# Expert selection, the last projection and the shared expert's groups put in another order at the end of an attention and expert layer

## The chip, the cores and the metric

The kernel runs on one core of a Trainium2 chip. The metric is the time of one execution on the device in microseconds (us), the median of several runs. TensorE (PE) multiplies matrices, VectorE (DVE) does most of the elementwise work, ScalarE (ACT) the activations and many copies, GpSimd (POOL) a part of the elementwise work and the indirect DMAs, and SyncE (SP) issues most DMAs.

## What is computed

One layer for x of shape (2, 2048, 256): attention with a memory that is updated by segments of 64 tokens, and then a mixture of 32 experts beside a shared expert. Abridged:

```python
# attention: 16 heads of 128, one step for each 64 tokens
scores = where(causal, q k^T / sqrt(128), -inf)
att_dot = softmax(scores) @ v
att_mem = sigma(q) @ mem / (sigma(q) @ z)          # sigma = elu + 1
delta = v - sigma(k) @ mem / (sigma(k) @ z)
mem += sigma(k)^T @ delta;  z += sum(sigma(k))
x = x + (beta * att_mem + (1 - beta) * att_dot) @ Wo      # on layernorm(x)

# experts, on n = layernorm(x), 4096 tokens
scores = sigmoid(n @ gate_w.T); sc = scores + gate_bias
groups = the 2 best of 4 groups of 8 experts, by the sum of their two best sc
topk_idx = the 4 best sc in these groups; weights = 2 * scores / sum(scores)
# each expert takes its first CAP = 64 tokens in the order of the tokens
out[token] += weight * (silu(n w1) * (n w3)) w2
shared = silu(n @ shared_gate) * (n @ shared_up) @ shared_down
x = x + out + shared
```

So of the tokens that choose an expert only the earliest 64 are kept. That makes the selection a search for the 64 earliest tokens of each of 32 experts.

## The kernel before

**Attention.** The 4096 tokens are 16 blocks (`NBLK`) of 128 tokens of both batches, and the 16 heads are 8 groups (`NG`) of 2. The main loop (`body` on each engine) goes over 16 blocks x 8 groups = 128 steps; step n = 8 x block + group, and the last block is steps 120 to 127. A step on PE: `numerators` for segment 0, the key projection of the next step (L1305), `attended_transposes` of the step before, `update` (L1364), the query projection, `numerators` for segment 1 (L1354), `probability_transposes`, the value projection, `key_transposes`, `update` for segment 1, `attend` (L1381), `scores` (L1328). DVE runs in its own fixed order: after `state(n, g, 0)` comes `sigma_k` of the next step (L875), `delta(n, 1)`, `sigma_q` (L868), `state(n, g, 1)` (L902), and PE's next `numerators` wait for that `state` (`mem_ready`). Pieces of the block before hang in between: in group 0 PE's output projection (`project_out`, L1410, 64 matmuls), in group 1 the residual and the statistics of the second layernorm, then the normalisation, the gate's chain of small operations, in group 7 its weights and `picks`.

**Picks.** For each block `picks` writes, for each expert and token, the value 4096 - token if the token chose the expert and 0 if not; a DMA stores them in DRAM (`picks`, 32 x 4096). The earliest 64 are then the 64 largest. `top8` finds eight of them by a MAX8 and strikes them out by a MATCH_REPLACE (which the trace shows as two instructions), and `ROUNDS` = 8 such rounds give 64. Before the change the selection comes after all blocks: four quarters of the tokens side by side on 128 partitions (`vq`, 1024 values, L1056 and L1057), then a merge of the four lists (`cm`, 256 values on 32 partitions).

**Shared expert.** It runs in 8 groups of 2 blocks. In the traces one group is, on PE, four `shared_half` (gate and up for two halves fc, L1462: banks bank_q, bank_k, chain_k, chain_q) and one `shared_down` (L1481), on ACT two `shared_silu` (L744), on DVE two `shared_mul` (L1044) and two `shared_add` (L1050) into `acc`, which holds x after attention. `FRONT` = 7 groups run before the experts, beside gate and selection, one after them. **Experts** run in 16 pairs: POOL gathers the rows of a pair, PE, ACT and DVE compute them (columns L1498, up L1510, down L1526), POOL adds them to DRAM (`expert_sums`) by indirect scatters (L586), two at a time, each two waiting for the two before. At the end SP loads the sums (`yt`, L431), DVE adds them to `acc` (`sum_add`, L1276, 4 pieces), SP stores the output (L436).

**What sets the order.** All of it is written out by hand. Each engine executes its list in order and waits on semaphores; SP's DMAs are issued in order too. `w_hi` and `w_lo`, the projection weights, share their memory with all buffers of the second half (`shared_place`), so the loads of shared weights and columns wait until the projections of some groups have run (`v_mm`). The expert weights lie over the attention's buffers (`expert_place`), so their loads wait for the end of attention.

## Time and profile before

| | us |
|---|---|
| median of 3 runs | 1823.87 |
| lowest and highest | 1821.38, 1825.12 |
| the profiled execution | 1825.59 |
| its span from first to last instruction | 1823.7 |

| engine | busy share of the span |
|---|---|
| PE matmuls | 95% |
| DVE | 66% |
| POOL | 50% |
| ACT | 44% |

The granted TensorE clock is 0.987 of full speed over the span. The profile page also cuts the span into 40 slices; PE is at 9 tenths or more in all but the first slice and three late ones (8 tenths in two, 3 tenths in the last). A time of a row is counted from the start of the span. A bracket behind a row of the timeline gives how long the engine had been idle before it, and who released it.

### The profile page before, as it was taken

What the parts mean: (1) busy time and instruction counts of PE and PEld (TensorE: products, weight loads), DVE (VectorE), ACT (ScalarE), POOL (GpSimd) and SP (SyncE); (2) the same over time, 40 slices, a digit from 0 to 9 for tenths busy, and PEclk for the clock granted to TensorE, in tenths of its full rate; (3) what the DMA queues carried; (4) which work ended last, traced back from release to release, by engine and by line L of the source; (5) the groups of instructions that cost most, each with busy time, mean ns of one, the idle gap of its engine ahead of it and who ended that gap; (6) DMA issues with size and microseconds to landing.
All of it is one profiled execution on the core that took longest, in us unless ns stands there. A gap on an engine that the chain in (4) does not pass through costs nothing. (4 is left out here: it accounts for less than half of the span.)

```text
span 1823.7 us, 45885 instructions
## 1 busy us (share of the span) xinstructions
PE 1728.6 (95%) x17990; PEld 1473.8 (81%) x17990; DVE 1208.0 (66%) x3996; ACT 805.4 (44%) x1936; POOL 916.7 (50%) x830
## 2 busy tenths in 40 slices
PE   6999999999999999999999999999999999989893
PEld 5788888888888888888888888888888888866451
DVE  6766757575767767575767677675767675663852
ACT  3544535353535445353535354453535354541040
POOL 3655646464646546464646455454646464530162
PEclk8999999999999999999999999999999999999997
DMA  4200000100000000001000000000010000046747
GB/s 152 70 22 25 15 19 8 32 8 25 15 15 25 15 25 15 19 8 32 8 22 18 15 25 15 25 15 19 8 32 8 15 25 9 25 148 188 207 80 202
DMA packets 83190, 75.23 MB, mean 41 GB/s; under 512 B 20992, under 2 KB 73808, under 8 KB 82720
## 3 DMA queue, kind: packets, MB, share of 16 engines
q1 hardware_dynamic: 79264, 65.89, 11.9%
q0 software_dynamic: 3680, 6.40, 1.9%
q8 instruction: 144, 2.36, 0.5%
q14 instruction: 70, 0.57, 0.1%
q10 hardware_dynamic: 32, 0.01, 0.0%
HBM read 47.78 MB, written 24.47 MB: 40 GB/s over the span
## 5 line engine op out<-in xcount | busy, mean ns | idle before, releaser
L489 POOL TENSOR_TENSOR step_place<-step_place 128x512 f32<-128x512 f32 x128 | 169.7, 1326 | 243.5 <-ACT step_place L645 243.5
L659 ACT ACTIVATE step_place<-chain_q,step_place 128x128 f32<-128x128 f32 x512 | 159.9, 366 | 275.2 <-DVE step_place L886 274.9
L902 DVE TENSOR_TENSOR step_place<-step_place,chain_k 128x258 f32<-128x258 f32 x256 | 107.7, 421 | 260.7 <-PE chain_q L1364 260.6
L525 POOL TENSOR_TENSOR step_place<-step_place 128x256 f32<-128x256 f32 x128 | 78.8, 615 | 313.5 <-DVE step_place L1079 313.5
L1410 PE MATMUL bank_o<-step_place 128*128 128x256 f32 x1024 | 226.0, 379 | 0.0
L480 POOL TENSOR_SCALAR step_place<-step_place 128x512 f32<-128x512 f32 x128 | 191.0, 1492 | 44.0 <-ACT step_place L639 43.9
L1410 PEld LDWEIGHTS bank_o<-step_place 128*128 128x128 f32 x1024 | 192.3, 190 | 25.4 <-issue 0.5
L474 POOL TENSOR_SCALAR step_place<-step_place 128x512 f32<-128x512 f32 x128 | 190.3, 1486 | 0.3 <-POOL step_place L498 0.3
L1354 PE MATMUL chain_k<-step_place 128*64 128x129 f32 x2048 | 166.0, 282 | 20.3 <-DVE step_place L902 20.2
L1364 PE MATMUL chain_k<-step_place 64*128 64x129 f32 x1024 | 181.4, 297 | 1.8 <-ACT step_place L659 1.1
L1364 PE MATMUL chain_q<-step_place 64*128 64x129 f32 x1024 | 181.6, 297 | 0.0
L1364 PEld LDWEIGHTS chain_k<-step_place 64*128 64x128 f32 x1024 | 132.4, 186 | 44.8 <-issue 42.3
L498 POOL TENSOR_TENSOR step_place<-step_place 128x512 f32<-128x512 f32 x128 | 164.6, 1286 | 0.0
L892 DVE SCALAR_TENSOR_TENSOR step_place<-chain_k,step_place 128x128 f32<-128x128 f32 x512 | 154.4, 342 | 6.1 <-DVE step_place L883 0.8
L1354 PE MATMUL chain_q<-step_place 128*64 128x129 f32 x2048 | 158.1, 273 | 0.0
L532 POOL TENSOR_TENSOR step_place<-step_place 128x256 f32<-128x256 f32 x128 | 78.5, 613 | 153.6 <-DVE step_place L1087 153.6
L652 ACT ACTIVATE step_place<-bank_k 128x512 f32<-128x512 f32 x128 | 76.7, 599 | 160.4 <-PE chain_q L1364 155.6
L1354 PEld LDWEIGHTS chain_k<-step_place 128*64 128x64 f32 x2048 | 109.2, 137 | 43.2 <-issue 29.3
L627 ACT ACTIVATE step_place<-bank_q 128x512 f32<-128x512 f32 x128 | 76.5, 598 | 136.0 <-PE bank_q L1305 136.0
L1364 PEld LDWEIGHTS chain_q<-step_place 64*128 64x128 f32 x1024 | 132.5, 186 | 0.0
L1354 PEld LDWEIGHTS chain_q<-step_place 128*64 128x64 f32 x2048 | 122.8, 136 | 0.0
L1305 PE MATMUL bank_k<-xt_hi,w_hi 128*128 128x256 f32 x512 | 116.6, 309 | 1.1 <-DVE xt_lo L860 1.1
(201 smaller groups left out, 4342.1 us busy)
## 6 DMA issues: line engine op xcount, KB each, us to landing
expert_place<-in_L_ffn_w_dram SPq DMA_DIRECT2D x24, 512.0 KB, 7.8
expert_sums<-zero SPq DMA_DIRECT2D x16, 272.0 KB, 5.1
expert_rows<-w_in SPq DMA_DIRECT2D x15, 288.0 KB, 2.2
step_place<-in_L_attn_x_dram SPq DMA_DIRECT2D x16, 256.0 KB, 3.0
x_res<-in_L_attn_x_dram SPq DMA_DIRECT2D x16, 256.0 KB, 3.2
x_rows<-w_in SPq DMA_DIRECT2D x16, 256.0 KB, 2.0
x_normed_t<-x1t SPq DMA_DIRECT2D x16, 256.0 KB, 2.0
shared_place<-x_normed_t SPq DMA_DIRECT2D x8, 512.0 KB, 8.2
```

The costliest lines, as they stand in the source:

```text
L474: nc.gpsimd.tensor_scalar(ex_q[:, :], ex_q[:, :], 1.0, None, ALU.min).then_inc(s["q_min"], 1)
L480: nc.gpsimd.tensor_scalar(ex_k[:, :], ex_k[:, :], 1.0, None, ALU.min).then_inc(s["k_min"], 1)
L489: nc.gpsimd.tensor_tensor(vb[:, :, :, :].rearrange("p s j d -> p s (j d)"), val[:, :, :, :].rearrange("p s j d -> p s (j d)"), rows.unsque ...
L498: nc.gpsimd.tensor_tensor(vo[:, :, :, :], val[:, :, :, :], vb[:, :, :, :], ALU.subtract).then_inc(s["vo_ready"], 1)
L525: nc.gpsimd.tensor_tensor(sm[:, :, :], sm[:, :, :], smx[:, :].unsqueeze(2).to_broadcast([128, T, SEG]), ALU.subtract).then_inc(s["s_shifte ...
L659: ins = nc.scalar.activation(am[:, par, seg, j, :], chain_q[:, j * ZC:j * ZC + DK], ACT.Copy, scale=rdq[:, seg, j:j + 1])
L892: ins = nc.vector.scalar_tensor_tensor(out=dl[seg][:, j, 0:DK], in0=chain_k[:, j * ZC:j * ZC + DK], scalar=rdk[:, seg, j:j + 1], in1=vb[:, ...
L902: ins = nc.vector.tensor_tensor(m, m, (chain_k, chain_q)[b][:, 0:HG * ZC].rearrange("p (j z) -> p j z", j=HG), ALU.subtract)
L1305: ins = mm(out, w[:, g, m, c, col], x[:, c, :, :].rearrange("p s t -> p (s t)"), start=i == 0, stop=i == len(parts) - 1)
L1354: ins = mm(out[ROWS[half], j * ZC:(j + 1) * ZC], sig[:, j, seg, b, :], mem[:, HG * g + j, b, :], start=True, stop=True)
L1364: ins = mm((chain_k, chain_q)[b][:, j * ZC:(j + 1) * ZC], ksig[ROWS[b], j, seg, :], dl[seg][ROWS[b], j, :], start=True, stop=True)
L1410: ins = mm(bank_o[:, b * D:(b + 1) * D], att[:, b * PIECES + i, :], wo[:, i, :], start=(i == 0 and b == 0), stop=(i == PIECES - 1), skip_g ...
```

## The change

It moves work of the last block and of the stages after it.

- **Selection in two parts.** The picks of the first 14 blocks (2 x 14 x 128 tokens as four parts of 896 on 128 partitions, `first_picks`) are loaded from DRAM at the start of the last block. Their 16 selection operations (`first_earliest(0)` to `(15)`, a MAX8 for even and a MATCH_REPLACE for odd numbers) stand inside the DVE steps of the last block: one ahead of `delta(n, 1)` (not in group 0), one ahead of `state(n, g, 1)`, and the last after attention. The four lists are copied beside the picks of block 14 in SBUF (`mid`, 512 values on 32 partitions), and 8 rounds over them run beside the last output projection. After the last block's gate 8 rounds over 320 values (`last_picks`) finish. The round trips of picks and lists through DRAM on POOL's queue go.
- **Shared loads earlier**, and the shared expert's group 0 is cut into other places; the last `update` and `state` for segment 1, and in step 127 the `delta` of segment 1 but for its query reciprocal, whose results nobody reads, are left out.
- **`FRONT` is 4.** Groups 0 to 3 run before the experts, 4 to 7 after them, with the `sum_add` between their operations, and the last two blocks are stored one by one.
- **SP's order** after the blocks: three quarters of x1 (`acc`), then the expert weights, between and after them the last block's stores.
- The picks of both batches lie on 64 partitions, so one transpose takes the place of two in each block.

```diff
-    FRONT = 7
+    FRONT = 4
+    PART = (NBLK - 2) // 2 * BLK
-    XSLOT = [0, 1, 2, 3, 4, 0, 1, 4]
+    XSLOT = [0, 1, 2, 4, 4, 0, 1, 2]
...
+        def load_picks():
+            sp.wait_ge(s["pickv_stored"], 16 * B * (NBLK - 2))
+            sp.wait_ge(s["v_mm"], NT - NG + 1)
+            for q in range(4):
+                b, part = divmod(q, 2)
+                at = b * S + part * PART
+                sp.dma_start(first_picks[q * E:(q + 1) * E, :], scratch["picks"][:, at:at + PART]
+                             ).then_inc(s["picks_arrived"], 16)
...
         def shared_loads():
-            sp.wait_ge(s["v_mm"], NT)
+            sp.wait_ge(s["v_mm"], NT - NG + 4)
...
+            load_columns(0)
+            load_columns(1)
+            sp.wait_ge(s["v_mm"], NT - NG + 6)
+            load_columns(2)
+            load_columns(3)
         blocks(sp, body)
...
+        sp.wait_ge(s["lists_kept"], 1)
+        sp.wait_ge(s["x1_stored"], 16 * NBLK)
+        for k in range(NK - 1):
+            load_blocks(acc, "x1", k, acc_arrived)
+        sp.wait_ge(s["att_ready"], NT)
+        for i in range(5):
+            load_batch(i)
         store_x1(NBLK)
+        for i in range(5, NB):
+            load_batch(i)
         store_columns(NBLK)
...
+        for g in range(5, NTG):
+            sp.wait_ge(s2["added"], 64 * (g - 4))
+            load_columns(g)
...
+        def first_earliest(k):
+            dve.wait_ge(s["list_step"], k) if k else dve.wait_ge(s["picks_arrived"], 16 * 4)
+            kept = first_kept[:, k // 2 * 8:k // 2 * 8 + 8]
+            ins = (nc.vector.max(kept, first_picks) if k % 2 == 0 else
+                   nc.vector.match_replace(out=first_picks, in_to_replace=kept,
+                                           in_values=first_picks, imm_value=-1.0))
+            ins.then_inc(s["list_step"], 1)
...
                     sigma_k(n + 1, (g + 1) % 2)
-                delta(n, 1)
+                if last and g:
+                    first_earliest(2 * g - 1)
+                delta(n, 1, nxt)
...
                     sigma_q(n + 1, (g + 1) % 2)
+                if last:
+                    first_earliest(2 * g)
...
-                state(n, g, 1)
+                if nxt:
+                    state(n, g, 1)
...
         blocks(dve, body)
+        dve.wait_ge(s["am_ready"], 2 * NT)
         attended(NT - 1, (NG - 1) % 2)
...
+        shared_mul(0, 0)
+        dve.wait_ge(s["pickv_ready"], NBLK)
+        dve.wait_ge(s["lists_kept"], 1)
+        for r in range(ROUNDS):
+            top8(last_picks, mid, r)
         residual(NBLK)
...
+        for g in range(FRONT, NTG):
+            shared_mul(g, 0)
+            if g > FRONT:
+                for k in range(TG):
+                    shared_add(g - 1, k)
+            if g == NTG - 2:
+                sum_add(0)
+            if g == NTG - 1:
+                sum_add(2)
+            shared_mul(g, 1)
+            if g == NTG - 2:
+                sum_add(1)
+            if g == NTG - 1:
+                sum_add(3)
+        dve.wait_ge(s2["y_added"], NK)
         for k in range(TG):
             shared_add(NTG - 1, k)
-        for k in range(NK):
-            sum_add(k)
```

Two places as each kernel's order has them. On DVE in step 121 (group 1 of the last block), from `sigma_k` to `state(n, g, 1)`, before (`bank_k` and `bank_q` hold projections, `chain_k` and `chain_q` the numerators):

```order
L875 SCALAR_TENSOR_TENSOR step_place<-bank_k,step_place 128x512 [waits k_min]
L883 RECIPROCAL step_place<-chain_k 128x2 [waits numk_mm]
L886 RECIPROCAL step_place<-chain_q 128x2 [waits numq_mm]
L892 SCALAR_TENSOR_TENSOR step_place<-chain_k,step_place 128x128 [waits rdk_ready]
...
L868 SCALAR_TENSOR_TENSOR step_place<-bank_q,step_place 128x512 [waits q_min,ln2_step]
L902 TENSOR_TENSOR step_place<-step_place,chain_k 128x2x129 [waits upd_mm]
```

and after (`shared_place` is `first_picks` here):

```order
L900 SCALAR_TENSOR_TENSOR step_place<-bank_k,step_place 128x512 [waits k_min]
L1056 MATCH_REPLACE shared_place<-shared_place 128x896 [waits list_step]
L913 RECIPROCAL step_place<-chain_k 128x2 [waits numk_mm]
L916 RECIPROCAL step_place<-chain_q 128x2 [waits numq_mm]
L922 SCALAR_TENSOR_TENSOR step_place<-chain_k,step_place 128x128 [waits rdk_ready]
...
L893 SCALAR_TENSOR_TENSOR step_place<-bank_q,step_place 128x512 [waits q_min,ln2_step]
L1055 MAX shared_place<-shared_place 128x8 [waits list_step]
L932 TENSOR_TENSOR step_place<-step_place,chain_k 128x2x129 [waits upd_mm]
```

Two selection operations of 896 values have come between, ahead of the `state` for which PE waits. On PE around the last output projection, before:

```order
L1381 MATMUL bank_v<-step_place 64x128 x2
L1462 MATMUL chain_k<-shared_place 128x512 [waits mem_ready]
L1462 MATMUL chain_k<-shared_place 128x512
L1391 MATMUL bank_a<-step_place 128x2x16x4 [waits att_summed]
L1391 MATMUL bank_a<-step_place 128x2x16x4 x3
L1462 MATMUL chain_q<-shared_place 128x512 x2
L1410 MATMUL bank_o<-step_place 128x256 [waits att_ready,pickv_ready]
...
L1481 MATMUL bank_s<-shared_place 128x256 [waits p2_sh_ready]
```

and after:

```order
L1439 MATMUL bank_v<-step_place 64x128 x2
L1449 MATMUL bank_a<-step_place 128x2x16x4 [waits att_summed]
L1449 MATMUL bank_a<-step_place 128x2x16x4 x3
L1468 MATMUL bank_o<-step_place 128x256 [waits att_ready,pickv_ready]
L1468 MATMUL bank_o<-step_place 128x256 x31
L1518 MATMUL chain_k<-shared_place 128x512 x2
L1518 MATMUL chain_q<-shared_place 128x512 x2
L1478 MATMUL bank_o<-ident,w_in 128x128 [waits x1_normed]
L1478 MATMUL bank_o<-ident,w_in 128x128 x3
L1486 MATMUL bank_o<-gwt,x1t 128x32 [waits x1t_ready]
```

The two shared halves have moved from around the last transposes to behind the projection, and the down projection of group 0 from ahead of the `x1` transposes to behind the logits.

## Rows read from the trace of the kernel before

**Rows 1.** Busy time by stretch: us, busy us (instructions) by engine, clock, DMA, GB/s
```profile
1783.00:1824.00 41.00, 10.59 (x32) 5.65 (x31) 11.92 (x8) 1.19 (x2) 6.24 (x4) 0.70 0.76 221
```

**Rows 2.** Chain of work that ended last: start us, us, what
```profile
1803.50 9.06 DMA expert_place<-expert_sums
...
1812.59 2.29 DVE shared_place L1276
```

**Rows 3.** Timeline of PE after attention: start us, us, what, count, idle before
```profile
1676.85 1.88 PE L1462 MATMUL bank_q<-shared_place 128*128 128x512 f32 x4
...
1687.17 1.88 PE L1462 MATMUL bank_q<-shared_place 128*128 128x512 f32 x4
1695.69 3.78 PE L1462 MATMUL bank_k<-shared_place 128*128 128x512 f32 x4 [6.64 <-DVE shared_place L1044]
...
1733.01 0.38 PE L1498 MATMUL bank_o<-ident,shared_place 128*128 128x128 f32 x2
...
1782.74 1.98 PE L1462 MATMUL bank_q<-shared_place 128*128 128x512 f32 x4 [0.47 <-ACT shared_place L786]
...
1790.71 1.99 PE L1481 MATMUL bank_s<-shared_place 128*128 128x256 f32 x8 [0.84 <-DVE shared_place L1044]
```

**Rows 4.** Timeline of PE, step 127 and the last output projection
```profile
1619.10 0.66 PE L1354 MATMUL chain_k<-step_place 128*64 128x129 f32 x8 [1.37 <-DVE step_place L902]
...
1623.57 3.75 PE L1462 MATMUL bank_q<-shared_place 128*128 128x512 f32 x4 [3.37 <-DMA shared_place<-x_normed_t]
1627.12 2.80 PE L1462 MATMUL bank_k<-shared_place 128*128 128x512 f32 x4
...
1640.36 13.98 PE L1410 MATMUL bank_o<-step_place 128*128 128x256 f32 x64
```

**Rows 5.** Granted clock by stretches of 2 us, columns as in Rows 1
```profile
1618.00:1620.00 2.00, 0.90 (x16) 0.89 (x16) 1.97 (x7) 0.00 (x0) 0.00 (x0) 1.00 0.84 223
...
1624.00:1626.00 2.00, 2.00 (x3) 0.72 (x3) 0.00 (x0) 0.00 (x0) 0.12 (x1) 0.50 1.03 397
```

**Rows 6.** Timeline of DVE, selection after attention: quarters, then the merge
```profile
1686.00 1.23 DVE L1056 MAX8 shared_place<-shared_place 128x8 f32<-128x1024 f32 x1 [8.21 <-DMA shared_place<-picks]
...
1688.58 1.23 DVE L1056 MAX8 shared_place<-shared_place 128x8 f32<-128x1024 f32 x1
...
1715.17 0.42 DVE L1056 MAX8 shared_place<-shared_place 32x8 f32<-32x256 f32 x1
...
1716.13 0.42 DVE L1056 MAX8 shared_place<-shared_place 32x8 f32<-32x256 f32 x1
```

**Rows 7.** DVE groups, steps 121 to 126: count, busy us, mean ns, idle before
```profile
L902 DVE TENSOR_TENSOR step_place<-step_place,chain_k 128x258 f32<-128x258 f32 x12 | 5.1, 422 | 7.5 <-PE chain_q L1364 7.5
...
L868 DVE SCALAR_TENSOR_TENSOR step_place<-bank_q,step_place 128x512 f32<-128x512 f32 x6 | 4.1, 691 | 2.7 <-POOL step_place L474 2.5 <-DVE tlist L978 0.2
...
L886 DVE RECIPROCAL step_place<-chain_q 128x2 f32<-128x2 f32 x12 | 1.9, 158 | 0.7 <-PE chain_q L1354 0.6
```

**Rows 8.** Timeline of DVE: a `state` of segment 0, and a gate operation
```profile
1557.60 0.42 DVE L902 TENSOR_TENSOR step_place<-step_place,chain_k 128x258 f32<-128x258 f32 x1 [0.77 <-PE chain_q L1364]
...
1612.69 1.28 DVE L966 TENSOR_SCALAR gm<-grp 128x8 f32<-128x8 f32 x1
```

**Rows 9.** Timeline of POOL beside the gate operation
```profile
1612.67 1.27 POOL L498 TENSOR_TENSOR step_place<-step_place 128x512 f32<-128x512 f32 x1
```

**Rows 10.** Timeline of DVE, last block: residual, gate scores, first operation after picks
```profile
1654.38 0.69 DVE L919 TENSOR_TENSOR w_in<-bank_o,x_res 128x512 f32<-128x512 f32 x1 [13.05 <-PE bank_o L1410]
...
1662.92 0.19 DVE L942 TENSOR_SCALAR eg<-eg 128x64 f32<-128x64 f32 x1 [0.32 <-ACT eg L732]
...
1670.86 0.66 DVE L1044 TENSOR_TENSOR shared_place<-shared_place,chain_q 128x512 f32<-128x512 f32 x1
```

**Rows 11.** SP's issues of expert weights, first and last
```profile
1661.14 1.49 SPq L382 DMA_DIRECT2D expert_place<-in_L_ffn_w_dram  x2
...
1701.78 2.34 SPq L385 DMA_DIRECT2D expert_place<-in_L_ffn_w_dram  x1
```

More of the change, by code:

```diff
@@ L326, in body @@
                 store_routing(blk)
+                if not last:
+                    store_picks(blk)
         def zero_part(blk):
@@ L1134, in _ @@
         blocks(dve, body)
+        dve.wait_ge(s["am_ready"], 2 * NT)
         attended(NT - 1, (NG - 1) % 2)
-        for fc in range(FC):
-            shared_mul(0, fc)
+        first_earliest(2 * ROUNDS - 1)
+        dve.wait_ge(s["list_step"], 2 * ROUNDS)
+        for q in range(4):
+            ins = nc.vector.tensor_copy(mid[:, q * CAP:(q + 1) * CAP],
+                                        first_kept[q * E:(q + 1) * E, :])
+        ins.then_inc(s["lists_kept"], 1)
+        shared_mul(0, 0)
[3 more added lines that the diff above has]
+            top8(last_picks, mid, r)
         residual(NBLK)
@@ L1141, in _ @@
         x1_apply(NBLK)
-        dve.wait_ge(acc_arrived[0], 16)
-        for k in range(TG):
-            shared_add(0, k)
-        shared_mul(1, 0)
+        shared_mul(0, 1)
         gate_scores(NBLK)
@@ L1189, in _ @@
         nc.vector.tensor_copy(tokf[:, :], bank_t[:, 0:NP]).then_inc(s2["idx_ready"], 1)
+        shared_mul(2, 1)
         for k in range(TG):
-            shared_add(5, k)
-        for fc in range(FC):
-            shared_mul(6, fc)
+            shared_add(1, k)
+        shared_mul(3, 0)
+        for k in range(TG):
+            shared_add(2, k)
+        shared_mul(3, 1)
         def weights(q):
@@ L1638, in _ @@
         pe.wait_ge(s2["yo_ready"], NP)
-        shared_up(NTG - 1, 0)
-        shared_up(NTG - 1, 1)
+        for g in range(FRONT, NTG):
+            shared_up(g, 0)
+            if g > FRONT:
+                shared_down(g - 1)
+            shared_up(g, 1)
         shared_down(NTG - 1)
```

228 lines of the change are left out of this document (103 added, 125 removed).

## The prediction

> **What bounds the kernel now.** I began with the page's 40 slices: PE is busy in nearly every one until the end of attention, so up to there only what delays PE costs time. Then I asked for busy time by stretch. In the last 41 us PE works 10.6 us [rows 1]. The chain that ended last says why: the sums of the experts come back by DMA, and four DVE additions and the output stores follow, the last addition starting at 1812.59 [rows 2]. The timeline of PE shows the rest: 6.64 us of waiting for DVE while it selects, the experts from 1733.01 to 1782.74, and only one shared group behind them [rows 3]. At step 127 PE waits 3.37 us for the shared loads, and what follows runs at half clock: 3.75 and 2.80 us for pieces that take 1.88 at full clock [rows 3, 4]. The granted clock is 0.50 there (1.2 of 2.4 GHz), and 1.00 around the wait of 1.37 us just before [rows 4, 5]. So a wait of 3.37 us cost 1.87 + 0.92 = 2.8 us more in clock; one of 6.64 us did so as well, its next piece taking 3.78 [rows 3].
>
> I add up PE's path from T0, the start of step 127's numerators (1619.10 before [rows 4]), to the start of the experts (T0 + 113.9 before [rows 3, 4]) and to the end.
>
> **The last block, T0 itself.** A selection round takes 2.58 us at 1024 values and 0.96 at 256 [rows 6], 2.11 ns a value: an estimate of 2.31 at 896, 1.50 at 512 and 1.10 at 320. Steps 121 to 126 each get one round, 6 x 2.31 = 13.9 us on DVE, all of it ahead of the `state` that releases PE. DVE's idle time takes some in: 7.5 us before `state`, of which six times 0.77 stands at segment 0, ahead of the new work, so 7.5 - 4.6 = 2.9; 2.7 before `sigma_q`; 0.7 at the reciprocals [rows 7, 8]. Left are 13.9 - 6.3 = 7.6 us. PE had no such idle time to hide them, so I count all. Bounds: 0 if slack elsewhere takes all, 13.9 if none of the idle time is of use. Step 120 has over 8 us of DVE idle time in its projection and hides its one operation.
>
> A second cost is small. A 128x8 TENSOR_SCALAR took 1.28 us and ended with the POOL operation beside it [rows 8, 9]; such operations of step 121's statistics and of step 126's gate are now pushed to where POOL works. Each can lose 0 to 1.3 us; I take 1.3 for both. T0 becomes 1619.1 + 7.6 + 1.3 = 1628.0.
>
> The Trainium skill (GPSIMD Engine Reference, Key points) says that GpSimd shares its SBUF interfaces with VectorE and that they contend for instructions in a two-port mode or with two SBUF inputs. That fits the 1.28 us [rows 8, 9]. MAX8 and MATCH_REPLACE are neither, so by the rule they lose nothing, as I count; were they held too, see the third rival.
>
> **Step 127 to the projection.** It took 1640.36 - 1619.10 = 21.3 us. Of this 3.4 was the DMA wait and 2.8 the clock; the loads now start some 30 us earlier, and both go. Four halves took 4 x 1.72 = 6.9 (a whole group, four halves and a down, takes 10.32, from 1676.85 to 1687.17 [rows 3], and a down has as many columns as two halves: 10.32 / 6); two of them move behind the projection. The other 8.2 us stays, less the last `update` (0.5), plus `first_earliest(14)` (1.1) ahead of the sum for which the transposes wait. 8.2 + 3.4 - 0.5 + 1.1 = 12.2. PE is idle for some 3 us of this, because no half covers the sum and the copy of the attention any more.
>
> **The projection** takes 14.0 [rows 4], to T0 + 26.2. Beside it DVE finishes the first list and runs 8 rounds of 512: about 1.8 + 0.7 + 12.0 = 14.5 us from T0 + 10.6, done at T0 + 25.1. It is covered by a margin of 1.1 us.
>
> **To the experts.** From projection to gate scores 8.5 us passed (1654.38 to 1662.92 [rows 10]); the two moved halves cover 3.4 of it, and PE waits about 1.6 for x1 and 0.7 for its copy. Its logits end at T0 + 33.4. Then come four downs and three ups of groups 0 to 3. A group's up is 6.9, its down 3.4: 4 x 3.45 + 3 x 6.9 = 34.5. Waits: `shared_mul(2, 1)` and the first add stand behind the index copies, 1.8; the last down behind its product, 0.8 [rows 3]; 0.4 for small matmuls. Experts start at T0 + 33.4 + 37.5 = T0 + 70.9. DVE meanwhile needs 7.9 us from gate scores to behind picks [rows 10], 8 x 1.10 for the rounds, 4 x 0.6 for shared work among them and 0.7 for indices: from T0 + 34.4 to T0 + 54.2, ahead of PE's token transposes at T0 + 57.6. So the selection no longer ends last; late next is PE itself. Before it was T0 + 113.9, with three groups (31.0 us) more in it: this stretch gains 113.9 - 31.0 - 70.9 = 12.0 us.
>
> The loads: SP issued the 24 expert weights from 1661.14 to 1701.78, some 43 us [rows 11]. They now start at about T0 + 23, behind 3 MB of x1, and end near T0 + 68; the first pair needs only the first batch. Hidden. Were that cover gone, a batch costs 43/8 = 5.4 us. The gathers (POOL) share the DMA engines with the last weights; PE reaches them 12 us after their issue.
>
> **Experts** take the same 49.7 us [rows 3]. **Four groups** follow: 4 x 10.32 + 0.8 = 42.1, to 91.8 after the experts' start. The sums came back first at 1803.5, 70.5 us after that start [rows 2, 3]; the first `sum_add` stands at 74.6. Each costs DVE 2.29 [rows 2] while PE has 10.32 a group: hidden. After the last down an addition (0.7) and a last store remain. The trace has 8.8 us from the last addition's end (1812.59 + 2.29) to 1823.7 for 1 MB behind other stores; now it is 0.25 MB. Bounds 2 and 8.8; I take 3.7. End at 96.2 after the experts' start; before, it was 1823.7 - 1733.0 = 90.7 with three groups less. Gain 90.7 + 31.0 - 96.2 = 25.5.
>
> **Sum without clock:** 1628.0 + 70.9 + 96.2 = 1795.1. **Clock:** PE now waits over 3 us at steps 121 (2.1 + 0.9) and 126 (the 1.37 of [rows 4] and 2.3 more), and 3 us before the projection; waits of 1.3 to 2 us stand elsewhere. Between 1.37 (no fall) and 3.37 (fall) the trace shows nothing, so each costs 0 to 2.8. Nearer to 3.37, I count three: 8.4. The short waits before the logits might add a fourth. Span 1803.5; the median of the runs lay 0.2 above the profiled span, so **1804**.
>
> **Rivals.**
> - *No falls of the clock, or DVE's idle time takes more in:* 1795. For it: the clock stayed at 1.00 over 1.37 us [rows 5].
> - *Tail not hidden:* the scatters or sums come late, because column loads for groups 5 to 7 share the engines with them. Then PE's groups wait or the four additions and stores stand at the end again: 4 x 2.29 = +9, 1813. Against it: 4 us of margin.
> - *Selection operations held by POOL like the 1.28 us one:* 12 operations losing 0.7 on average: +8, 1812. Against it: only the TENSOR_SCALAR kinds show it. Its likeness, that the selection still ends last before the token transposes, gives +4 to +8.
> - *Slower:* waits come in steps 121, 122, 125, 126 and 127, each about 10 us apart. If the clock didn't come back between them (after 1623.57 it took some 5 us of work), steps 121 to 127, 7 x 10.4 us of PE, would run at half clock: +73, less the 7.6 of waits they would hide and the 8.4 counted: 1804 + 57 = 1861. Work at half clock costs its own length again, so it decides once PE does some 28 us of work more at half clock than I count (the 20 us of gain and the 7.6 that would be hidden).
>
> **How the numbers follow.** Forecast (three falls, 1799 to 1809) 0.50; 1795 and below 0.15; late tail 0.10; held or still last selection 0.15; slower 0.06; the rest, between 1814 and no change, 0.04. The range 1793 to 1814 takes in the first four but for their edges. A measurement of this kernel can tell about 0.2%, 3.6 us, from no change. Faster 0.91, same 0.03, slower 0.06.
>
> **What would show it.** In the profile after: T0 at about 1628 plus clock (each selection step's PE wait on `state`, 1 to 3.5 us); no DMA wait at step 127; the MAX8 rounds of 512 ending before PE's projection; no PE wait on DVE above 2 us between logits and experts; the experts 71 us after T0 without clock loss; the sum additions between products of groups 6 and 7; 3 to 5 us after the last down. Wrong would be: PE waiting for DVE in every step with the clock at 0.5 throughout, PE waiting for weights or gathered rows, or sums that arrive after the last down.

## The result, and the profile after

The changed kernel takes 1802.7 us (median of four runs, 1800.9 to 1805.3), against 1824.3 us for the kernel before on the same chip. The ratio is 0.9886, with a 95% interval of 0.9868 to 0.9903: 1.1% faster. The profiled execution is the slowest of the four, 1805.3 us with a span of 1803.5, and the other three spans are 1799.1 to 1801.8. The sum in the prediction had come to a span of 1803.5 and a time of 1804, so that it meets the profiled span to the digit is chance, and it lies 1.3 us above the median.

Busy time of the last 40.5 us, which answers to [rows 1] (same columns):

```profile
1763.00:1803.50 40.50, 35.48 (x114) 21.20 (x112) 18.40 (x19) 3.58 (x6) 3.82 (x3) 1.00 0.73 220
```

PE works 35.5 us of this end where it had worked 10.6, and its clock is 1.00 where it was 0.70. (The low clock of the kernel before stood behind 1799 us, after PE's last work, and cost nothing.) The chain that ended last no longer goes through the DMA of the experts' sums, as in [rows 2], but through the last shared group (start us, us, what):

```profile
1795.47 0.69 DVE shared_place L1090
...
1796.20 1.99 PE bank_s L1537 x8
1798.20 1.74 PE bank_v L1537 x8
...
1799.96 0.69 DVE shared_place L1096
```

The timeline of PE from step 122 on, which answers to [rows 3, 4] (start us, us, line, what, count, and in brackets the idle time before it with what ended it; L1412 is the numerators, L1449 the last attention transposes, L1468 the projection, L1518 a shared half, L1478 the transposes of x1, L1544 those of the selected tokens, L1537 a shared down projection, L1554 the experts' columns):

```profile
1566.24 1.13 PE L1412 MATMUL chain_k<-step_place 128*64 128x129 f32 x8 [2.66 <-DVE step_place L932]
...
1582.34 0.85 PE L1412 MATMUL chain_k<-step_place 128*64 128x129 f32 x8 [2.52 <-DVE step_place L932]
...
1631.73 0.66 PE L1412 MATMUL chain_k<-step_place 128*64 128x129 f32 x8 [2.45 <-DVE step_place L932]
...
1632.76 1.98 PE L1518 MATMUL bank_q<-shared_place 128*128 128x512 f32 x4
...
1642.90 0.66 PE L1449 MATMUL bank_a<-step_place 128*128 128x128 f32 x4 [2.58 <-DVE step_place L941]
...
1644.46 15.57 PE L1468 MATMUL bank_o<-step_place 128*128 128x256 f32 x64 [0.90 <-ACT step_place L700]
...
1665.19 0.66 PE L1478 MATMUL bank_o<-ident,w_in 128*128 128x128 f32 x4 [1.74 <-DVE w_in L868]
...
1693.50 0.29 PE L1544 MATMUL bank_o<-ident,shared_place 32*64 32x16 f32 x4
1695.50 1.97 PE L1537 MATMUL bank_s<-shared_place 128*128 128x256 f32 x8 [1.71 <-DVE shared_place L1096]
...
1707.02 0.38 PE L1554 MATMUL bank_o<-ident,shared_place 128*128 128x128 f32 x2
...
1756.67 1.98 PE L1518 MATMUL bank_q<-shared_place 128*128 128x512 f32 x4 [0.47 <-ACT shared_place L811]
...
1796.20 1.99 PE L1537 MATMUL bank_s<-shared_place 128*128 128x256 f32 x8 [1.44 <-DVE shared_place L1090]
```

So T0, the start of step 127's numerators, is 1631.7 (before 1619.1); the experts start 75.3 us behind it (before 113.9, with three shared groups more in that stretch), and the end of the span is 96.5 us behind that (before 90.7, with three groups fewer). The largest wait of the kernel before, 6.64 us for the selection, is gone. The long waits are now for the attention chain of DVE, in steps that carry two operations of the selection.

The granted clock (last column but two of these rows) shows where those waits cost a second time, as [rows 5] did for the kernel before:

```profile
1566.00:1568.00 2.00, 1.76 (x16) 1.61 (x16) 1.59 (x6) 0.00 (x0) 0.37 (x1) 0.50 0.00 0
1582.00:1584.00 2.00, 1.66 (x17) 1.36 (x17) 1.68 (x6) 0.00 (x0) 0.28 (x1) 0.67 0.00 0
...
1632.00:1634.00 2.00, 2.00 (x19) 1.26 (x15) 1.76 (x7) 0.79 (x3) 0.61 (x1) 1.00 0.00 0
1644.00:1646.00 2.00, 1.54 (x4) 1.30 (x5) 1.93 (x6) 0.93 (x4) 0.00 (x0) 0.53 0.15 12
1668.00:1670.00 2.00, 2.00 (x6) 1.61 (x5) 1.70 (x12) 1.30 (x2) 0.00 (x0) 0.50 1.13 322
```

There are four falls to 1.2 GHz: at the starts of steps 122 and 123, at the projection, and behind the logits. Read by stretches of 1 us, the first lasts 6.8 us and the others 3.4 us each. Behind the wait of 2.45 us at 1631.73 the clock stays at 1.00.

DVE's timeline, which answers to [rows 6] and to the additions of [rows 2] (L1102 and L1103 are a round of the merge, L949 the residual, L1231 the copy of the indices, L1323 an addition of the experts' sums, L1090 a shared product):

```profile
1645.36 0.67 DVE L1102 MAX8 shared_place<-shared_place 32x8 f32<-32x512 f32 x1
...
1656.59 0.66 DVE L1103 MATCH_REPLACE8 shared_place<-shared_place 32x512 f32<-32x512 f32 x1
1660.12 0.69 DVE L949 TENSOR_TENSOR w_in<-bank_o,x_res 128x512 f32<-128x512 f32 x1 [2.87 <-PE bank_o L1468]
...
1693.91 0.17 DVE L1231 CAST shared_place<-bank_o 128x16 uint32<-128x16 f32 x1 [4.42 <-PE bank_o L1544]
...
1782.95 2.28 DVE L1323 TENSOR_TENSOR shared_place<-shared_place,expert_place 128x2048 f32<-128x2048 f32 x1
...
1793.27 2.29 DVE L1323 TENSOR_TENSOR shared_place<-shared_place,expert_place 128x2048 f32<-128x2048 f32 x1
1795.47 0.68 DVE L1090 TENSOR_TENSOR shared_place<-shared_place,chain_q 128x512 f32<-128x512 f32 x1
1796.06 2.29 DVE L1323 TENSOR_TENSOR shared_place<-shared_place,expert_place 128x2048 f32<-128x2048 f32 x1
```

The merge ends 2.87 us before the projection, and the selection is ready 4.42 us before PE wants it: neither is on the path any more. The additions stand between products, as the change says. The third of them puts off the last product (1795.47), which the last down projection waits for: 1.44 us in place of 0.84.

### The profile page after: what moved, and what is told of

Read it like the earlier page. It is cut to its first block, busy times and chain, and to the rows that moved or that the text cites. A ratio compares the mean times of both kernels' runs of the same rounds, so it can differ in the third digit from the quotient of the medians.

```text
span 1803.5 us, 45871 instructions
## 1 busy us (share of the span) xinstructions
PE 1729.2 (96%) x17966; PEld 1476.5 (82%) x17966; DVE 1216.9 (67%) x4020; ACT 805.9 (45%) x1936; POOL 912.7 (51%) x822
## 3 DMA queue, kind: packets, MB, share of 16 engines
q1 hardware_dynamic: 79664, 66.32, 12.2%
## 4 chain that ended last, share of the span: by engine, by line
PE 77%; DVE 15%; issue 3%; ACT 2%; POOL 2%; DMA 1%; DVEq 0%; SPq 0%; POOLq 0%; ACTq 0%
PE bank_o L1468 12%; PE bank_k L1363 10%; PE bank_q L1363 8%; PE bank_v L1373 7%; PE chain_k L1422 6%; PE chain_k L1412 6%; PE chain_q L1412 5%; PE bank_s L1386 3%; PE bank_a L1449 3%; PE bank_a L1439 3%; DVE step_place L932 2%; PE bank_s L1457 2%; PE bank_k L1395 2%; POOL step_place L520 1%; DVE step_place L900 1%
## 5 line engine op out<-in xcount | busy, mean ns | idle before, releaser
L1468 PE MATMUL bank_o<-step_place 128*128 128x256 f32 x1024 | 227.6, 381 | 0.9 <-ACT step_place L700 0.9
L1468 PEld LDWEIGHTS bank_o<-step_place 128*128 128x128 f32 x1024 | 193.3, 191 | 26.5 <-issue 1.1
L1412 PE MATMUL chain_k<-step_place 128*64 128x129 f32 x2048 | 166.4, 282 | 28.1 <-DVE step_place L932 28.0
L1412 PE MATMUL chain_q<-step_place 128*64 128x129 f32 x2048 | 158.8, 274 | 0.0
L1412 PEld LDWEIGHTS chain_k<-step_place 128*64 128x64 f32 x2048 | 109.3, 137 | 52.0 <-issue 39.1
L1412 PEld LDWEIGHTS chain_q<-step_place 128*64 128x64 f32 x2048 | 123.3, 137 | 0.0
```

What stands on the lines that cost most here:

```text
L1412: ins = mm(out[ROWS[half], j * ZC:(j + 1) * ZC], sig[:, j, seg, b, :], mem[:, HG * g + j, b, :], start=True, stop=True)
L1468: ins = mm(bank_o[:, b * D:(b + 1) * D], att[:, b * PIECES + i, :], wo[:, i, :], start=(i == 0 and b == 0), stop=(i == PIECES - 1), skip_g ...
```

## The experiments

My theory was the prediction's: the operations in steps 121 to 126 cost what exceeds DVE's idle time there, plus the clock that their waits cost; the early loads, the selection off the path and the hidden additions earn the rest. The operations' cost, the loads and the additions are tested below, each against a rival. That the two-part selection and `FRONT` = 4 earn the rest is read from the traces alone; no run takes one of them back. Differences from the changed kernel are between medians of the same chip where it ran beside (e4, e6, e7), and otherwise between the ratios to the kernel before, times 1824 us. A ratio's interval is some 3 us to either side.

### What the operations cost in the attention steps: e1_ops_16, e2_ops_448

```
-            ins = (nc.vector.max(kept, first_picks) if k % 2 == 0 else
+            ins = (nc.vector.max(kept, first_picks[:, 0:16]) if k % 2 == 0 else
...
-                   nc.vector.match_replace(out=first_picks, in_to_replace=kept,
-                                           in_values=first_picks, imm_value=-1.0))
+                   nc.vector.match_replace(out=first_picks[:, 0:16], in_to_replace=kept,
+                                           in_values=first_picks[:, 0:16], imm_value=-1.0))
```

The second has 448 in place of 16. Both leave out a part of the choice among the earlier picks; they measure time only.

> The sixteen selection operations read and write 16 columns of the list in place of 896, so most of the choice among the earlier picks is left out; every instruction, wait and place stays. In the changed kernel one takes 1.08 us on VectorE, and step 127 began at 1631.7 us. Theory (the prediction's): these operations fill VectorE's idle time of steps 121 to 126 (6.3 us in the kernel before) and lengthen the block by the rest, and the two falls of the clock at the starts of steps 122 and 123 come from the waits that they make. With operations of about 0.2 us, 13 of them before step 127 fit into the idle time: step 127 begins near 1619.5 us, neither fall is there, and the median is 11 to 13 us under the changed kernel's, near 1790.5. Rival: the steps are held by something else that moved (the loads of the shared weights and columns in steps 123 to 126, the picks' loads at the block's start): step 127 still begins at 1628 or later, and the median is at most 4 us lower.

> The same with 448 columns in place of 896 (half of the earlier picks are left out of the choice). One operation should take 0.62 us. Theory: what counts is what exceeds VectorE's idle time. Of the 13 operations before step 127, 13 x 0.62 = 8.1 us stand against an idle time of 6.3 us, so the block is 2 us longer than in the kernel before, and the waits of TensorE are shorter than those that brought the falls: step 127 begins near 1621.5, and the median is 9 to 11 us under the changed kernel's. Rival: the cost goes with the width, without a threshold: half of what 16 columns give, 5 to 6 us under the changed kernel's, and at least one of the two falls stays.

Measured: 1790.7 us and 1797.8 us, ratios 0.9821 (0.9805 to 0.9838) and 0.9859 (0.9843 to 0.9876): 11.9 and 4.9 us under the changed kernel. The start of step 127 with 16 columns, and then the start of step 122 and the first half of step 127 with 448 columns (timelines of PE):

```profile
1618.40 0.66 PE L1412 MATMUL chain_k<-step_place 128*64 128x129 f32 x8 [1.52 <-DVE step_place L932]
```

```profile
1564.95 0.66 PE L1412 MATMUL chain_k<-step_place 128*64 128x129 f32 x8 [1.77 <-DVE step_place L932]
...
1623.90 3.41 PE L1518 MATMUL bank_q<-shared_place 128*128 128x512 f32 x4
```

With 16 columns (0.17 us an operation) step 127 begins 77.5 us behind the second half of step 120, as in the kernel before (77.3); in the changed kernel it is 90.6. That settles what delayed the block: the time of the operations, and none of the loads that moved with them. With 448 columns (0.62 us) it is 82.2, so the two mechanical costs, overflow of the idle time and clock, are both there. What I had wrong is the clock: I had expected none behind waits under 2 us, but a fall to 0.50 follows the wait of 1.77 us (0.57 over the stretches of 2 us from 1566 us on), another one that of 1.98 us before step 127 (the half at 1623.90 takes 3.41 us and not 1.98), and a third stands at the projection. In its profiled run this kernel is 8.8 us under the changed kernel's profiled run and in the medians 4.9. The theory's 9 to 11 fails, and the rival comes nearer, with its 5 to 6 us and one of the two falls left. The growth of the block is 0.3, 4.9 and 13.3 us at 16, 448 and 896 columns, and with the falls (about 1.6 us, and 4.4) taken off some 3.3 us at 448 and 8.9 at 896. Half of the 8.9 would be 4.4, the theory's overflow 1.8: the rows lie between the two and don't decide for either.

### Where the operations are free: e6_early_ops

```
+                if last and g == 0:
+                    for k in range(6):
+                        first_earliest(k)
+                if last and g == 4:
+                    first_earliest(13)
                 delta(n, 1, nxt)
...
+                if last and g == 0:
+                    for k in range(6, 13):
+                        first_earliest(k)
...
+        first_earliest(2 * ROUNDS - 2)
         first_earliest(2 * ROUNDS - 1)
```

> The changed kernel with its selection operations, at full width and all of them, in other places: six in step 120 ahead of the reciprocals of its second half (in the changed kernel VectorE waits there 6.7 us while TensorE runs the first half of an output projection), seven in step 120 ahead of the second update of the state (it waits 7.5 us there beside the projection's second half, with one operation done), one in step 124 and two behind the attention. Theory: what an operation costs is set by its place alone. 6 x 1.08 = 6.5 us and 7 x 1.08 = 7.6 us lie in those two waits, so steps 121 to 126 run as with the 16-column operations: step 127 begins near 1618.5 us in place of 1631.7, the falls at steps 122 and 123 are gone, and the median is 11 to 13 us under the changed kernel's, near 1791. Rival: the picks' loads (issued from 1530.0 us) land late for the first of them, and VectorE's idle time ahead of the first wait begins only at 1535, so the six overrun it and the step: 4 to 8 us lower only.

> The changed kernel once more, on the chip of the three kernels that run with it, to have them side by side. Both theories: 1801 to 1805 us, with falls of the clock at the same four places, give or take one.

Measured: 1790.9 us (1790.5 to 1791.8) beside 1801.7 us (1800.4 to 1806.9) for the changed kernel: 10.8 us less with all of the work at full width, just short of the 11 to 13 of the theory. DVE in step 120, and PE at step 127:

```profile
1550.54 1.09 DVE L1055 MAX8 shared_place<-shared_place 128x8 f32<-128x896 f32 x1
...
1552.19 0.42 DVE L932 TENSOR_TENSOR step_place<-step_place,chain_k 128x258 f32<-128x258 f32 x1 [0.56 <-PE chain_q L1427]
```

```profile
1618.51 0.66 PE L1417 MATMUL chain_k<-step_place 128*64 128x129 f32 x8 [1.37 <-DVE step_place L932]
```

Thirteen operations fill the two waits of step 120 to within 0.56 us, and step 127 begins 77.3 us behind step 120's second half, the very figure of the kernel before, with its very wait of 1.37 us [rows 4]. The picks arrived in time, so the rival falls. No fall of the clock is left between step 120 and step 127; one of 6.8 us stands at the projection, from 1628.8 us on, behind a wait of 1.64 us. The price of an operation was its place.

The second profile of the changed kernel (1806.9 us, the slowest of its four, outside the 1801 to 1805 expected; the median is inside) has falls at the same four places, but of other lengths: 3.4 us at steps 122 and 123, and 6.8 us at the projection and behind the logits. Two stretches of its projection:

```profile
1644.00:1646.00 2.00, 2.00 (x6) 1.55 (x6) 1.93 (x5) 0.00 (x0) 0.00 (x0) 0.50 0.60 103
1646.00:1648.00 2.00, 2.00 (x7) 1.55 (x6) 1.90 (x6) 0.00 (x0) 0.00 (x0) 0.50 1.03 378
```

### The early loads: e5_late_loads, e9_late_loads_8

```
-            sp.wait_ge(s["v_mm"], NT - NG + 4)
+            sp.wait_ge(s["v_mm"], NT)
...
-            sp.wait_ge(s["v_mm"], NT - NG + 6)
+            sp.wait_ge(s["v_mm"], NT)
```

> The changed kernel with the shared expert's weights and the columns of its first four groups loaded from the last value projection on (near 1626 us), where the kernel before loads them, and not in steps 123 to 126. Theory: the first shared half of step 127 waits for its weights, by 3.4 us as in the kernel before, and the clock falls there (2.8 us more of work at the lower one), of which a part lies in the time by which VectorE's attention chain is the later one (TensorE waits 2.6 us for it before the last attention transposes, and this wait shrinks): 3 to 6 us slower. Rival: VectorE's chain bounds step 127, and TensorE's wait for the load only takes the place of its wait for VectorE: within 1 us of the changed kernel.

Measured: 1803.4 us, ratio 0.9886 (0.9869 to 0.9902), the ratio of the changed kernel to the last digit. The rival has the number, but not the reason. PE:

```profile
1629.36 0.66 PE L1412 MATMUL chain_k<-step_place 128*64 128x129 f32 x8 [2.44 <-DVE step_place L932]
...
1630.77 3.58 PE L1518 MATMUL bank_q<-shared_place 128*128 128x512 f32 x4 [0.30 <-DMA shared_place<-x_normed_t]
...
1642.58 0.65 PE L1449 MATMUL bank_a<-step_place 128*128 128x128 f32 x4 [2.58 <-DVE step_place L941]
```

DVE in step 127, at its first `state`, in this kernel and then in the changed one:

```profile
1635.55 0.42 DVE L932 TENSOR_TENSOR step_place<-step_place,chain_k 128x258 f32<-128x258 f32 x1 [3.07 <-PE chain_q L1422]
```

```profile
1635.88 0.42 DVE L932 TENSOR_TENSOR step_place<-step_place,chain_k 128x258 f32<-128x258 f32 x1 [1.03 <-PE chain_q L1422]
```

The wait for the columns is 0.30 us and not the 3.4 of the theory, since the selection's operations have put off step 127 until the loads have landed: it begins 5.6 us behind the first of these loads' issues (1623.76), in e9_late_loads_8 below only 3.6 us behind. The clock does fall there (a half of 3.58 us). This isn't hidden beneath DVE's chain: DVE waits 2.0 us longer for PE, and the projection begins 14.77 us behind T0 in place of 12.73. That PE's wait before the last transposes stays at 2.58 us means that DVE's part begins where PE's `update` ends, and passes the delay on. The fall, 1.7 of these 2.0 us, need not be the loads': e4_filled, whose loads are early, has one at the same place. That the times agree all the same comes, in the profiles, from falls elsewhere: here the block has one of 3.4 us in place of two, and none follows the logits. With such differences from one execution to the next, the medians can't show 2 us.

> The kernel that runs beside it (e8_mul_ahead) with the shared weights and columns loaded from the last value projection on, the edit that made no difference to the changed kernel. Theory: there the load's latency was hidden because the selection's operations had made step 127 begin 6.1 us behind the issue of these loads; with step 127 beginning at 1618, about 6 us behind the projection as in the kernel before, the first shared half waits 2 to 3.4 us for its columns and the clock falls there, of which TensorE's slack before the last attention transposes (none is left once a shared half fills it) hides nothing: 3 to 6 us slower than e8_mul_ahead. Rival: the early loads are worth nothing in any of these kernels, since VectorE's chain through step 127 is the longer one: within 1 us.

Measured (the kernel beside it is described below): 1787.1 us against 1782.7, 4.4 us slower, ratios 0.9807 (0.9791 to 0.9823) and 0.9782 (0.9766 to 0.9799).

```profile
1621.68 3.75 PE L1521 MATMUL bank_q<-shared_place 128*128 128x512 f32 x4 [2.44 <-DMA shared_place<-x_normed_t]
```

Here step 127 begins at 1618.1, and the wait is back at 2.44 us with a half at half clock (3.75 us, as in [rows 4]). The projection begins 16.71 us behind T0 in place of 11.86, and those 4.9 us are the wait of 2.44 and as much again for the clock. So the early loads are worth 4.4 us in a kernel whose step 127 isn't late; in the changed kernel the rows show 0.3 us of waiting for them, and the medians nothing.

### The additions at the end: e3_sums_last

```
-            if g == NTG - 2:
-                sum_add(0)
-            if g == NTG - 1:
-                sum_add(2)
             shared_mul(g, 1)
-            if g == NTG - 2:
-                sum_add(1)
-            if g == NTG - 1:
-                sum_add(3)
+        for k in range(NK):
+            sum_add(k)
```

> The changed kernel with its four additions of the experts' sums (2.28 us each) put together behind the last multiplication of the shared groups, as in the kernel before; nothing else differs. In the changed kernel one of them already stands there, beneath the last down projections (1796.2 to 1799.9 us). Theory: the other three are 6.8 us on the path of the end, less 1.4 us of down projection left over that still hides one of them, less the 0.6 us by which the third made the last multiplication late: 4.8 us slower, plus up to 2 us since the stores of the outputs start later and land together: 4.8 to 7 us slower, median near 1808. Rival: the stores set the end, and move one for one with the last addition: over 7 us slower.

Measured: 1814.0 us, ratio 0.994 (0.9921 to 0.9959): 9.9 us slower, the rival's number. From the chain of that kernel, and its busy time near the end:

```profile
1798.36 6.70 DVE shared_place L1323 x3
```

```profile
1806.00:1808.00 2.00, 0.00 (x0) 0.00 (x0) 0.37 (x1) 0.00 (x0) 0.00 (x0) 0.50 1.04 348
1808.00:1810.00 2.00, 0.00 (x0) 0.00 (x0) 0.00 (x0) 0.00 (x0) 0.00 (x0) 0.50 1.03 344
```

DVE's last addition (a `shared_add`) ends at 1806.4 against 1800.6, 5.7 us later, 0.7 of which lay ahead of the tail already; 5.0 agrees with my 4.8. But the span ends 6.2 us behind it and not 2.9. The outputs (six stores of 512 KB, two of 256, four of 128: 4.2 MB) move at 344 GB/s with the DMA engines full, so by these numbers they need 12 us from the first addition's end (1798.5), whatever DVE does later: 1798.5 + 12 and 2 for landing is the 1812.6 of the span. So the stores don't move one for one with the last addition, as the rival had it, but with the first. In the changed kernel the first stores go out at 1785.3. There too the DMA engines are full at the end (share 1.01 from 1798 to 1802 us), with half of the output to be moved from 1796 us on; the third addition one group earlier (e8_mul_ahead below) brings the end from 3.6 to 3.4 us behind the last down projection, no more.

### Filling PE's waits: e4_filled, e7_both, e8_mul_ahead

```
+        shared_half(0, 1, 0)
         attended_transposes(NT - 1, (NG - 1) % 2)
         pe.wait_ge(s["pickv_ready"], NBLK)
         project_out(0, PIECES, NT)
-        shared_half(0, 1, 0)
         shared_half(0, 1, 1)
+        shared_up(1, 0)
         x1_transposes(NBLK)
         logits(NBLK)
         shared_down(0)
-        shared_up(1, 0)
-        pick_transposes(NBLK)
         shared_up(1, 1)
+        pick_transposes(NBLK)
...
+        shared_mul(2, 1)
+        for k in range(TG):
+            shared_add(1, k)
         dve.wait_ge(s2["sel_mm"], 1)
```

`first_earliest(14)` stands behind the last attention addition as in e6_early_ops, and `sum_add(2)` behind `sum_add(1)`.

> The changed kernel with TensorE's waits behind the attention filled: one shared half (1.98 us) moved ahead of the last attention transposes, where it waits 2.6 us; two more halves ahead of the last norm's transposes, where it waits 1.7 us; the last MAX8 behind the last attention addition, which it holds up by 1.1 us; the multiplication and two additions of group 1 and 2 ahead of the copies of the indices (TensorE waits 1.7 us for them); and the third addition of the experts' sums one group earlier (TensorE waits 0.6 us for it). Theory: TensorE is the bound from the last projection to the experts, since VectorE's selection stands idle for 4.4 us at its end: 2.0 + 1.7 + 1.7 + 0.6 = 6.0 us of wait go, and the fall at the projection or at the logits with them if the wait is what brings it (1.6 us each): 6 to 9 us under the changed kernel's. Rival: two halves more ahead of the last norm's transposes make the gate, and with it the selection, late by what they fill, and the selection is last again: 2 to 4 us lower only.

Measured: 1797.5 us (1794.8 to 1798.8), 4.2 us under the changed kernel beside it. That is just above the rival's 2 to 4 and under the theory's 6 to 9, and neither story is right as told. The waits of 2.6, 1.7 and 1.7 us are gone, the projection takes 14.05 us, and the selection isn't last; but the clock now falls in step 127 (from 1628 us on), and PE stops at another place:

```profile
1675.73 3.67 PE L1537 MATMUL bank_s<-shared_place 128*128 128x256 f32 x8 [3.08 <-DVE shared_place L1090]
```

With two halves done earlier PE comes to the down projection of group 1 while its product on DVE still stands behind the third round of selection. That wait of 3.08 us brings a fall of its own (3.67 us in place of 1.99).

> Both of the edits together: operations in step 120, waits of TensorE filled. Theory: they lie one after the other on the path, and their gains add up: 16 to 21 us under the changed kernel's, median near 1784. Rival: with the step's delay gone the fill has less to do (TensorE's wait for the last attention is 1.7 us with narrow operations, in place of 2.6): under 15 us.

Both edits: 1786.2 us (1784.9 to 1786.9), 15.5 us less, between the theory's 16 and the rival's 15. The two gains alone add up to 15.0, so they do add up, and each was smaller than forecast. The wait of 3.08 us is still there, at 1665.16, this time with the clock at 1.00. The next kernel takes it away:

```
         shared_mul(1, 0)
+        shared_mul(1, 1)
         dve.wait_ge(s["pickv_ready"], NBLK + 1)
...
-            if r == 2:
-                shared_mul(1, 1)
-            if r == 6:
+            if r == 4:
                 shared_mul(2, 0)
```

> Both edits together as before, and the multiplication of group 1's second half put ahead of the rounds of selection, the first of group 2 behind the fifth round in place of the seventh. With both edits TensorE stood still for 3.1 us before the down projection of group 1 (1662.1 to 1665.2 us), since this multiplication sat behind the third round. Theory: TensorE is the bound there and VectorE's list is ready 4 us before TensorE wants it: the wait goes, and the median is 2.5 to 3.1 us under the 1786.2 us of both edits. Rival: the rounds of selection end 0.3 us earlier at best, so the transposes of the list take over as the wait: under 1 us.

Measured: 1782.7 us (1781.8 to 1783.2), ratio to the kernel before 0.9782 (0.9766 to 0.9799); by the ratios 2.4 us under both edits and 17 to 19 us under the changed kernel (0.9876 and 0.9886). By the medians it is 3.5 us under both edits, and the wait itself is 2.7 us shorter, which is what the theory says; the times can't tell it closer.

```profile
1618.73 0.66 PE L1415 MATMUL chain_k<-step_place 128*64 128x129 f32 x8 [1.38 <-DVE step_place L932]
...
1630.59 14.05 PE L1471 MATMUL bank_o<-step_place 128*128 128x256 f32 x64 [0.90 <-ACT step_place L700]
...
1663.13 1.97 PE L1540 MATMUL bank_s<-shared_place 128*128 128x256 f32 x8 [0.39 <-DVE shared_place L1096]
...
1685.40 0.38 PE L1557 MATMUL bank_o<-ident,shared_place 128*128 128x128 f32 x2
```

The wait is 0.39 us. The experts start 66.7 us behind T0 (75.3 in the changed kernel), and from 1500 us to the end of PE's work the granted clock is 1.00 throughout. This version is 2.2% faster than the kernel before, and computes all of it.

## Why the prediction was right, point by point

The sum came out as forecast, and so did its three large terms. Parts of all three are right only because errors cancel.

- **T0.** Predicted 1628.0 and two falls of the clock, 1633.6; measured 1631.7. From the second half of step 120 on the block grew by 90.6 - 77.3 = 13.3 us. From one step's numerators to the next the two falls take 2.8 + 1.6 = 4.4 us of it (half of the time that PE worked in them is 4.8). The 8.9 left are the 7.6 + 1.3 of the prediction, but not placed as it had them. The prediction put the idle time of six steps in one sum. In the kernel before it stands almost wholly in steps 123 and 124 (2.0 and 2.4 us ahead of `sigma_q` and of the second `state`; none in 121, 0.3 in 122, 0.8 in 125, 0.2 in 126). So these two steps took their two operations for nothing, and steps 121, 122, 125 and 126 grew by 2.8, 2.9, 1.2 and 2.0 us. The second `state` of step 124 before (DVE):

```profile
1595.89 0.42 DVE L902 TENSOR_TENSOR step_place<-step_place,chain_k 128x258 f32<-128x258 f32 x1 [1.28 <-PE chain_q L1364]
```

  e1_ops_16 shows the sum from the other side: with the operations' time taken away, the growth is gone. The round of 2.31 us was right.
- **The small cost beside POOL.** In step 121 a TENSOR_SCALAR of 128x2 took 1.17 us and ended with the POOL operation beside it, while a MATCH_REPLACE of 128x896 took its 1.08 us beside one (DVE's rows, then POOL's):

```profile
1559.26 1.08 DVE L1056 MATCH_REPLACE8 shared_place<-shared_place 128x896 f32<-128x896 f32 x1
...
1562.14 1.17 DVE L848 TENSOR_SCALAR v_x<-mv_x 128x2 f32<-128x2 f32 x1
...
1573.95 1.20 DVE L862 SCALAR_TENSOR_TENSOR rs_x<-b_x,rs_x 128x2 f32<-128x2 f32 x1
...
1578.36 1.25 DVE L860 SCALAR_TENSOR_TENSOR b_x<-a_x,v_x 128x2 f32<-128x2 f32 x1
```

```profile
1558.51 1.28 POOL L538 TENSOR_TENSOR step_place<-step_place 128x512 f32<-128x512 f32 x1
...
1562.01 1.28 POOL L529 TENSOR_TENSOR step_place<-step_place 128x512 f32<-128x512 f32 x1 [0.75 <-ACT step_place L672]
```

  So the rival of held selection operations falls: all thirteen before T0 took 1.07 to 1.09 us. But the cost wasn't small. Three operations are held in steps 121 and 122 that weren't in the kernel before (the three above), each by 1.0 to 1.1 us; in step 126 two are held, as in the kernel before. That is some 3 us, if all of it reaches PE, in place of 1.3, and it explains why steps 121 and 122 grew by more than a round of 2.31 us. The overflow of the idle time is then nearer 5.9 than 7.6: the two terms are off by 1.7 us to opposite sides.
  The Trainium skill (GPSIMD Engine Reference, Key points) says that GpSimd contends with VectorE's instructions in a 2-port mode or with two SBUF inputs. The prediction counted MAX8 and MATCH_REPLACE as neither, and the trace agrees, with 1.08 us beside POOL as without.
- **From T0 to the projection.** Predicted 12.2, measured 12.7, but the reason given for 6.2 of the gain, the early loads, is wrong for this kernel: with late loads (e5_late_loads) the wait is 0.3 us and not 3.4. The step that failed is "the loads now start some 30 us earlier, and both go". Both went, but because the operations of the selection had made step 127 late. With that delay gone the same loads are worth 4.4 us (e9_late_loads_8).
- **Projection and merge.** The merge ended 25.5 us behind T0 (predicted 25.1). The margin was 2.87 us and not 1.1, of which 1.6 is the projection's own fall (15.57 us against 13.98).
- **To the experts.** Predicted 70.9 + 2.8 for the clock = 73.7; measured 75.3. The waits were 1.74 for x1, 0.69 for its copy, 1.71 and 0.84 for the products and additions (predicted 1.6, 0.7, 1.8, 0.8). The falls cost 1.6 us at the projection and 1.7 behind the logits, which the prediction named as a possible fourth: together 0.5 more than the 2.8 counted. The other 1.1 us lie in the 0.5 of step 127 and between projection and logits.
- **The end.** Predicted 96.2 behind the experts' start, measured 96.5: 49.65 for the experts, 43.3 for the four groups and their last product (predicted 42.1), 3.6 behind the last down projection (3.7 + 0.7). `sum_add(2)` put off the last product by 0.6 us, which I had missed. e3_sums_last shows that additions out of cover cost 9.9 us, close to the 9 of the rival; that rival had it all on DVE, and the stores' transfer takes nearly half.
- **The clock.** Predicted three falls of 2.8 us, behind the waits of steps 121 and 126 and at the projection. The first and the third came. Behind step 126's wait (2.45 us, where 3.7 had been forecast) there was none, and two others came, behind step 122's wait and behind the logits. Half of the time that PE worked in them is 3.1 + 1.7 + 1.6 + 1.7 = 8.1 us against 8.4. That places and sizes were off and the sum right is luck: in the second profile the last two falls are twice as long and the first half as long.
- **The slower rival**, a clock that doesn't come back between steps, didn't occur: it came back within 6.8 us in every trace.

What isn't settled is which waits bring a fall. The wait of 2.44 to 2.45 us at the start of step 127 stands in five traces with the same work ahead of it: a fall follows in e4_filled and e5_late_loads, none in the changed kernel's two profiles nor in e3_sums_last. The wait of 2.66 us before step 122 has none in e5_late_loads and one in the other four, and the wait of 3.08 us before the down projection of group 1 has one in e4_filled and none in e7_both. The wait of 1.73 us for x1 has one in the changed kernel and none in e1_ops_16 or e6_early_ops. Nothing that I ran tells these cases apart. The kernels without these waits behind step 120 (e7_both but for one, and e8_mul_ahead) have no fall up to the end of PE's work.

## What to carry to other kernels

Before work is spread evenly over steps, look for the one step in which its engine stands idle because another has a long job: two waits of 6.7 and 7.5 us in one step took thirteen operations for nothing, while the same operations, two to a step, cost 11 us. Add up idle time step by step: what two steps have left over doesn't help the four that have none. Taking away a wait ahead of the bounding engine moves the next product or addition in program order onto its path, so follow the order one product further before counting the gain, and undo each part of a change on its own: of three tested here, one changed nothing that the medians show while the others were in place. Additions that release stores are due by the transfer time of the output behind them, not by the end of the computation.

## What the runs showed of the hardware

- A fall of the clock at the same place of the same program lasted 3.4 us in one execution and 6.8 in another, and the same wait is followed by one or not. The changed kernel with its four falls ranges over 4.4 and 6.5 us in four runs each; the last version, whose profile has none in its last block or behind it up to the end of PE's work, over 1.4 us. But e5_late_loads, with three falls in its profile, ranges over 1.0 us, so that the falls make the spread isn't shown.
- A fall can follow a short wait: falls followed waits of 1.77 and 1.98 us in e2_ops_448 and one of 1.64 us in e6_early_ops, while the clock stayed at 1.00 over 3.08 us in e7_both.
- Stores of the output ran at 344 to 348 GB/s from one core with all of its DMA engines busy (share 1.03 to 1.04), so the 4.2 MB of output need some 12 us (an estimate from that rate).
- An operation of two to eight values a partition on DVE can take 1.17 us instead of 0.17 beside an elementwise operation of POOL; the selection's operations, a hundred times as wide, took 1.08 us beside it as without.
